# A binarised 3x3 convolution on 64x64 images: two output rows from four products, and the 3x3 sums of sizes on 64 partitions through memory

## What is computed

```python
def _L1_conv_ref(x, kernel, bias):             # x here is _gn(x): group norm
    xp = jnp.pad(x, ((0, 0), (1, 1), (1, 1), (0, 0)))
    bin_k = _sign_pm1(kernel)                  # 3 x 3 x 256 x 256, +1 or -1
    alpha = jnp.mean(jnp.abs(kernel), axis=(0, 1, 2))
    bin_x = _sign_pm1(xp)                      # v > 0 gives +1, else -1
    beta = jnp.mean(jnp.abs(xp), axis=3, keepdims=True)
    K = lax.reduce_window(beta, 0.0, lax.add, (1, 3, 3, 1), (1, 1, 1, 1), 'VALID') / 9
    conv = lax.conv_general_dilated(bin_x, bin_k, window_strides=(1, 1), padding='VALID', ...)
    return conv * (K * alpha) + bias
...
x = x + _L1_conv_ref(_gn(x), L1_conv_kernel, L1_conv_bias)
```

## Time and profile before

| | |
|---|---|
| median of 3 runs | 4247.38 us (4243.71 to 4248.18) |
| the profiled execution | 4246.04 us, span 4244.2 us |
| layer 1 in the span | first DMA issued at 3553.4 us, to the end |
| TensorE, VectorE, ScalarE, GpSimd busy, whole span | 3872.8, 3561.1, 2423.4, 569.8 us |

### The profile page before, as it was taken

The page is one execution under the profiler, slowest core; times in us unless marked ns, Lnnn a source line. Parts: engine busy times, 40 slices in busy tenths (PEclk is TensorE's granted clock), DMA queues, the critical chain, the costliest instruction groups (busy, mean ns, idle before and its releaser), DMA issues. The chain is left out here.

```text
span 4244.2 us, 94584 instructions
## 1 busy us (share of the span) xinstructions
PE 3872.8 (91%) x38382; PEld 2480.9 (58%) x38382; DVE 3561.1 (84%) x2896; ACT 2423.4 (57%) x5027; POOL 569.8 (13%) x480
## 2 busy tenths in 40 slices
PE   3899999999999999999999999999999985888988
PEld 1466666666666666666666666666666663333333
DVE  2799899989998899899989998999899993556554
ACT  4666666666666666666666666666666622333332
POOL 0011111111111111111111111111111110222222
PEclk9999999999999999999999999999999996999999
DMA  4454455445544554555445544554454433222321
GB/s 129 108 115 100 101 126 123 99 103 119 120 100 104 120 119 99 109 123 119 99 101 125 124 99 101 121 129 99 100 106 104 79 57 133 89 90 90 136 92 60
DMA packets 308092, 453.20 MB, mean 107 GB/s; under 512 B 33456, under 2 KB 239024, under 8 KB 301872
## 3 DMA queue, kind: packets, MB, share of 16 engines
q0 software_dynamic: 95168, 197.15, 25.9%
q1 hardware_dynamic: 212464, 249.71, 19.4%
HBM read 245.38 MB, written 67.11 MB: 74 GB/s over the span
## 5 line engine op out<-in xcount | busy, mean ns | idle before, releaser
L982 DVE TENSOR_TENSOR pv<-val,wsum 128x2048 f32<-128x2048 f32 x800 | 1810.3, 2283 | 11.1 <-PE ps_add L791 11.0
L791 PEld LDWEIGHTS ps_add<-ident,pv 128*128 128x128 f32 x12800 | 1399.7, 142 | 325.7 <-issue 220.7
L791 PE MATMUL ps_add<-ident,pv 128*128 128x128 f32 x12800 | 1525.0, 275 | 39.5 <-DVE pv L982 31.0
L746 PE MATMUL ps_om<-xdw,omw 128*32 128x256 f32 x13824 | 884.4, 389 | 124.7 <-ACT hat L579 109.1
L746 PEld LDWEIGHTS ps_om<-xdw,omw 128*32 128x32 f32 x13824 | 395.0, 111 | 431.7 <-ACT hat L579 120.8
L470 POOL DMA_DIRECT2D wsum<-prod x192 | 226.0, 1255 | 2688.6 <-DVE wsum L935 2688.6
L577 ACT ACTIVATE hat<-ps_om,omb 128x256 f32<-128x256 f32 x576 | 275.4, 478 | 537.0 <-PE ps_om L746 537.0
L935 DVE TENSOR_TENSOR prod<-hat,mwy 128x1536 f32<-128x1536 f32 (+1 forms) x384 | 525.2, 1395 | 59.0 <-DMA wsum<-prod 42.5
L1530 PE MATMUL ps_c<-c_sgn,c_ksgn 128*128 128x512 bf16 x2304 | 518.7, 384 | 2.5 <-DVE c_res L1647 2.5
L542 ACT ACTIVATE tri<-tri,gn_tri 96x512 f32<-96x512 f32 (+3 forms) x812 | 473.5, 647 | 6.0 <-DMA tri<-in_zeros_dram 0.5
L921 DVE TENSOR_TENSOR mwy<-hat,msk 128x768 f32<-128x768 f32 x288 | 274.1, 952 | 223.7 <-ACT hat L591 223.5
(11 more groups left out here) (102 smaller groups left out, 2791.2 us busy)
## 6 DMA issues: line engine op xcount, KB each, us to landing
wsum<-prod POOLq DMA_DIRECT2D x160, 768.0 KB, 6.9
tri<-in_x_dram SPq DMA_DIRECT2D x725, 128.0 KB, 2.9
win<-in_x_dram SPq DMA_DIRECT2D x144, 256.0 KB, 3.3
xres<-in_x_dram POOLq DMA_DIRECT2D x128, 256.0 KB, 9.0
x<-xres SPq DMA_DIRECT2D x128, 256.0 KB, 4.1
c_x<-x SPq DMA_DIRECT2D x8, 4096.0 KB, 13.0
out_dram<-c_x SPq DMA_DIRECT2D x32, 1024.0 KB, 4.0
acc<-in_x_dram POOLq DMA_DIRECT2D x14, 1024.0 KB, 5.6
```

The source lines that it names most:

```text
L746: mm = nc.tensor.matmul(ps_om[G * q:G * q + G, (par + i) % 2, 0:TOK], omw[:, h, comp, :], xdw[:, j % 2, h, q, :], start=h == 0, stop=h == ...
L791: mm = nc.tensor.matmul(ps_add[:, tb, c, :], pv[:, (j + uv) % PBUF, c, P * tb:P * tb + P], consts["ident"][:, :], start=uv == 0 and c % 4 ...
L982: nc.vector.tensor_tensor(pv[:, (j + uv) % PBUF, :, :].rearrange("p c (r w) -> p c r w", w=W), val[:, :, SR * j + u:SR * j + u + SR, v:v + ...
```

## The change

Only `layer1` changes. Three things go together.

**Products.** Two output rows are made of four products in place of six (for each column tap and input half). For a pair of output rows, the four input rows d0 to d3 give four planes: d0 - d2 and d1 - d3 (`over2`), d1 + d2 and d2 - d1 (`mid`, SUM and DIFF). They are made on VectorE in bf16 (`planes`), and weighed with four sets of weights `kw` that are made once. The products of `mid` are wanted in both rows with different signs: TensorE writes them to PSUM (`middle`, 12 matmuls), ScalarE copies them to `res`, one with its sign turned (`keep_middle`), TensorE then adds the outer products onto what stands in PSUM (`outside`, 12 matmuls), and VectorE adds `res` and PSUM (`combine`). The multiplication with `box` is a step of its own (`weigh`).

**Units.** A chunk is 16 rows (8 pairs, 1024 pixels); an image has 4 chunks and 8 units. `ps_p` has 3 slots of 2 banks, `res` 5 buffers. Loads, stores and signs go by chunk; `sgn` holds one image, and `planes` copies what the products read. All images are written out, with no loop.

**Sizes.** `mean_size` runs twice an image. It takes 8 products with 32 output channels each, four to different groups of 32 partitions of one bank, and adds the two halves itself (no `add_halves`). One partition of each group then holds 8 rows of the image's mean sizes. Four DMAs store them to a padded image in memory (`store_beta`), three DMAs load it back as 64 rows on 64 partitions, shifted by 0, 1 and 2 rows (`load_rows`), VectorE makes the sums in four steps of 66 or 64 elements (`box_sums`), a DMA stores the result, and another spreads it to 128 partitions (`spread_box`, 2 MB).

```diff
+    PAIRS = 8
+    CHUNKS = H // (2 * PAIRS)
+    CT = 2 * PAIRS * W
     UNITS = CHUNKS * CH
-    BANKS = 4
+    SLOTS, RES = 3, 5
...
+                def store_beta(n, half):
+                    sp.wait_ge(beta_out, 2 * n + half + 1)
+                    for i in range(BLOCKS):
+                        r0 = 1 + BW // W * (BLOCKS * half + i)
+                        sp.dma_start(beta_d[n % 2:n % 2 + 1, r0:r0 + BW // W, 1:1 + W],
+                                     beta[32 * i:32 * i + 1, half, :].rearrange("p (r w) -> p r w", w=W)).then_inc(beta_stored, 16)
+                def load_rows(n):
+                    sp.wait_ge(beta_stored, 16 * 2 * BLOCKS * (n + 1))
+                    for dr in range(3):
+                        sp.dma_start(rows[:, dr, :], beta_d[n % 2, dr:dr + H, :]).then_inc(rows_loaded, 16)
...
+                for n in range(NI):
+                    more = n + 1 < NI
+                    store_chunk(n, 0)
+                    if more:
+                        store_beta(n + 1, 0)
+                    refill(n, 0)
+                    if more:
+                        store_beta(n + 1, 1)
+                        load_rows(n + 1)
+                    store_chunk(n, 1)
+                    if more:
+                        store_box(n + 1)
+                    refill(n, 1)
+                    if more:
+                        spread_box(n + 1)
...
+                def keep_middle(i):
+                    act.wait_ge(mid_full, i + 1)
+                    if i >= RES:
+                        act.wait_ge(added, i - RES + 1)
...
+                    nc.scalar.activation(v[:, :, 0, :], total, ACT.Copy)
+                    nc.scalar.activation(v[:, :, 1, :], diff, ACT.Copy, scale=-1.0).then_inc(mid_kept, 1)
...
+                for i in range(UNITS * NI):
+                    n, u = i // UNITS, i % UNITS
+                    more = n + 1 < NI
+                    for w in weighed_at(i):
+                        affine(w)
+                    if more and u < 2:
+                        sizes(n + 1, u)
+                    if i + 1 < UNITS * NI:
+                        keep_middle(i + 1)
+                    if more and u in (2, 3):
+                        sizes(n + 1, u)
+                    if more and u in (2, 4):
+                        keep_beta(n + 1, u // 2 - 1)
...
+                def middle(i):
+                    n, u = i // UNITS, i % UNITS
+                    pe.wait_ge(v_made, 3 * (CHUNKS * n + u // CH + 1))
+                    if i >= SLOTS:
+                        pe.wait_ge(rows_done, i - SLOTS + 1)
+                    plane(n, u, DIFF, ps_p[:, i % SLOTS, 0, :], False)
+                    plane(n, u, SUM, ps_p[:, i % SLOTS, 1, :], False).then_inc(mid_full, 1)
+                def outside(i):
+                    n, u = i // UNITS, i % UNITS
+                    pe.wait_ge(mid_kept, i + 1)
+                    plane(n, u, FIRST, ps_p[:, i % SLOTS, 0, :], True)
+                    plane(n, u, LAST, ps_p[:, i % SLOTS, 1, :], True).then_inc(rows_full, 1)
...
+                for i in range(UNITS * NI):
+                    if i + 1 < UNITS * NI:
+                        middle(i + 1)
+                    outside(i)
+                    if i // UNITS + 1 < NI and i % UNITS in (2, 4):
+                        mean_size(i // UNITS + 1, i % UNITS // 2 - 1)
...
+                for n in range(NI):
                     for u in range(UNITS):
                         i = UNITS * n + u
+                        for w in weighed_at(i):
+                            weigh(w)
+                        if n == 0 and u == 2:
+                            box_sums(0)
+                        if u == 0:
+                            planes(n, CHUNKS - 1)
+                        elif n + 1 < NI:
+                            if u <= CHUNKS:
+                                signs(n + 1, u - 1)
+                            if u == 5:
+                                box_sums(n + 1)
+                            if u >= 5:
+                                planes(n + 1, u - 5)
+                        combine(i)
```

More of the change, by code:

```diff
@@ L1367, in layer1 @@
         xb = sb("c_x", [P, 2, CH, HW])
[L1368 to L1377, removed]
+        sgn = sb("c_sgn", [P, CH, PAD, PAD], BF16)
+        over2 = sb("c_over2", [P, CHUNKS, CH, 2 * PAIRS, PAD], BF16)
+        mid = sb("c_mid", [P, CHUNKS, 2, CH, PAIRS, PAD], BF16)
+        kw = sb("c_kw", [P, 4, CH, 3, C], BF16)
+        size = sb("c_size", [P, CH, HALF])
+        beta = sb("c_beta", [P, 2, BW])
+        rows = sb("c_rows", [H, 3, PAD])
+        down = sb("c_down", [H, PAD])
+        box_rows = sb("c_box_rows", [H, W])
+        box = sb("c_box", [P, 2, HW])
+        res = sb("c_res", [P, RES, CT])
         mean256 = sb("c_mean", [P, P])
@@ L1389, in layer1 @@
[L1389 to L1410, removed]
+        spare = xb[:, 1, :, :].rearrange("p h t -> p (h t)")
@@ L1499, in _ @@
+                affine(UNITS * NI - 1)
             @block.tensor
@@ new lines, in plane @@
+                def plane(n, u, which, at, more):
+                    t, oh = u // CH, u % CH
+                    for h in range(CH):
+                        for kx in range(3):
+                            if which in (SUM, DIFF):
+                                src = mid[:, t, which, h, :, kx:kx + W]
+                            else:
+                                r0 = 0 if which == FIRST else 1
+                                src = over2[:, t, h, r0:2 * PAIRS:2, kx:kx + W]
+                            first, last = h == 0 and kx == 0, h == CH - 1 and kx == 2
+                            mm = nc.tensor.matmul(at.rearrange("p (r w) -> p r w", w=W), kw[:, which, h, kx, P * oh:P * oh + P],
+                                                  src, start=first and not more, stop=last, skip_group_check=True)
+                    return mm
@@ new lines, in _ @@
+                pe.wait_ge(kern_step, KERN_STEPS)
+                middle(0)
+                pe.wait_ge(alpha_kept, 1)
+                for oh in range(CH):
+                    for i in range(2):
+                        mm = nc.tensor.matmul(ps_b[:, 0, oh:oh + 1], alpha[:, C * i + P * oh:C * i + P * oh + P],
+                                              mean256[:, 0:1], start=i == 0, stop=i == 1)
+                mm.then_inc(alpha_full, 1)
+                pe.wait_ge(scale_made, 1)
+                for half in range(2):
+                    mean_size(0, half)
```

388 lines of the change are left out of this document (199 added, 189 removed).

## The result

The changed kernel takes 4035.07 us (median of 4, 4028.21 to 4037.11) against 4246.31 for the one before: ratio 0.950, 95% interval 0.9484 to 0.9517, 211 us less. The prediction said 4042, 4000 to 4112. The profiled execution spans 4026.4 us and took 4028.21.

What follows compares the result with a forecast made beforehand. TensorE sets the second layer's pace: 3596.5 + 64 x 5.24 + 14 x 1.9, plus stops of 11.5 + 11.6 + 5 x 7.9, gives 4021; the end makes 4034, clock 6 and 1.8 around the span 4042 us, range 4000 to 4112.

Steps and rivals of the forecast that it cites:

- The choice between the two bounds: VectorE's `planes`: 4.6 us at float32 two-input pace or 2.4 at `c_ksgn`'s pace; the forecast took 2.4.
- a turn of 6.04 us: Port shared by VectorE and GpSimd, in units making planes: weigh 1.22 + planes 2.42 + GpSimd 2.4, against TensorE's 5.24.
- the one behind `sizes`: TensorE's 3.1 us wait in the unit where weigh, affine, both `sizes` and the copies follow each other.
- the one at unit 5: TensorE's 2.2 us wait for `combine`, queued on VectorE behind `box_sums`, which stands 7.2 us for the memory trips.
- the one in unit 6: TensorE's 1.0 us wait in unit 6, from the port turn.
- the two of 0.8: TensorE's 0.8 us waits: for `keep_middle` in the previous image's last unit with planes, and in unit 1 behind GpSimd.
- the clock's 6 us: TensorE's lower clock after gaps of 3 us, one an image: half of 1.7 us may come back, +6 in all.
- Slower planes: Rival: `planes` on VectorE at one element a cycle, port turn 8.3 us, image about 66 us, total 4135; chance 0.08.
- Slow memory trips: Rival: each small DMA lands in 4 us rather than 2, adding 4 us an image, total 4070; chance 0.10.
- No lock: Rival: the lock between VectorE and GpSimd costs nothing, as GpSimd falls between the steps; total 4014; chance 0.05.
- No overlap of the array's quarters: Rival: `mean_size` products on TensorE's array quarters don't overlap, about 10 us an image, total 4115; chance 0.02.
- A low clock throughout: Rival: TensorE stays at 1.2 GHz, a matmul 0.436 us, an image 87.5, the whole 4300; chance 0.02.

Runs made afterwards that it cites:

- run 1: Changed kernel with the 3x3 sums (`box_sums`) at unit 6 of VectorE's program, not unit 5: 4008.69 us, ratio 0.9447.
- run 2: Changed kernel with ScalarE's copies (`keep_middle`) ahead of the two `sizes` steps in units 0 and 1, not behind them: 4015.32 us, ratio 0.9459.
- run 7: Changed kernel with GpSimd adding only 64 of a unit's 1024 elements, the rest of the residual left out: 4004.89 us, ratio 0.9431.
- run 9: Changed kernel with each chunk's planes made once more in row order, into a spare place nobody reads: 4139.95 us, ratio 0.9757.
- run 4: Changed kernel with the middle products made twice, so 36 matmuls a unit as before the change: 4148.08 us, ratio 0.9776.
- run 5: Changed kernel without sizes and their sums for images 1 to 7, all weighed with the first image's sums: 3958.02 us, ratio 0.9324.
- run 6: Kernel before the change without sizes and their sums for images 1 to 7, using the first image's sums: 4116.16 us, ratio 0.9687.

## Why the prediction was right

The mechanism came out: TensorE still sets the pace, its products cost what was said, and an image loses the rest in the stops that were named, for the reasons that were named. That the total lies within 7 us is in part luck, since the start and the images were wrong in opposite directions.

**TensorE's terms.** The forecast had 24 matmuls a unit at 0.218 us. A piece of 12 stands at 2.78 to 2.85 us with its drain, and the next starts 2.62 after it; 48 in a row take 10.69. `mean_size` was two calls of 1.9 us and is 1.85 and 1.90 in the chain. Right.

**VectorE's terms.** `combine` was 1.22 (1.216 measured), `weigh` alone 1.22 (1.22 to 1.23). The planes were 0.62 + 0.62 + 1.18 = 2.42; from the first one's start to the start of `combine` behind them are 2.40 (3762.19 to 3764.59). The choice between the two bounds, by bytes read per ns, came out. The Trainium skill's page "VectorE: DVE Perf Modes" (The perf-mode tier table) has this rate, and the trace now shows it: 2112 elements in 1.25 us.

**The port.** Forecast was a turn of 6.04 us, with `weigh` stretched and `combine` not. Measured is 5.71. From the last plane's end to the addition's end are 2.21 us and not its 2.36, from there to `weigh`'s end 1.08 and not 1.22, and the next plane starts 0.08 before that end: each step saves some 0.1 us by following another. The mechanism was right and the term 0.3 us too large.

**An image.** Forecast was 53.6 us; by the starts of `mean_size` in the chain, 3676.28 and 3940.89, five images are 264.6 us, 52.9 each. Of the stops in the list, the one behind `sizes` was 3.1 and is 2.50, the one at unit 5 was 2.2 and is 1.65 to 1.77, the one in unit 6 was 1.0 and is 0.64, and the two of 0.8 are 0.24 each, or one of them none. That is 5.0 to 5.4 read off. But idle time is counted from the drain's end, so a stop costs 0.23 more than it reads (2.85 against 2.62), and the stops come to some 6.0 to 6.5 where 7.9 was said. The port's shorter turn is one cause. It is not the cause at unit 5, where VectorE stands for `c_rows`: there the mean sizes land in 1.7 us and not 2.0, and it stands 6.8 to 6.9 where 7.2 was said. Runs 1, 2 and 7 show that the sums, the copies and the port each count.

**The first image.** The forecast gave the first two images losses of 11.5 and 11.6 us. Measured, nearly all of it falls on one: from the first `mean_size` for the second image (3611.7) to the first for the third (3676.3) are 64.6 us, some 19 above its own work, and the next period has the 52.4 of the others. Half of it is the stop of 9.4 us that is shown with the profile, and the lower clock behind it about 4; run 1, in which that stop is 4.1 us, has 58.1. The forecast gave the memory trips 7.2 us in every image and did not see that in the first one they stand in the queue behind a store and a load that waits for it. The two together lose some 26 us, of which about 4 are the clock's, where 23 was said without the clock.

**The start was too small.** From the layer's first DMA to the stream of units were 43.1 us in the forecast (3596.5 - 3553.4) and are 47.2 measured (3595.2 - 3548.0). The weights landed in 10.45 (11 said), and the steps on VectorE took 9.8 (10.0). What was missed is TensorE's low clock, where the sum used full speed:

```profile
3573.72 5.28 PE L1614 MATMUL ps_p<-c_mid,c_kw 128*128 128x512 bf16 x12 [6.90 <-DVE c_over L1688]
...
3583.01 3.38 PE L1599 MATMUL ps_b<-c_size,c_mean 128*32 128x512 f32 x16 [1.29 <-ACT c_size L1528]
```

The granted clock from 3540 to 3595 is 0.59. The rows take 5.28 us in place of 2.6 and 3.38 in place of 1.9, and the second `mean_size` 3.64: 6 us more, of which the other terms, too large together, took back 2. In the earlier trace rows the same effect stood in plain sight, and the sum priced it only for the images.

**The clock in the images.** The forecast allowed 6 us, by the earlier trace rows, whose stop it read as some 4 us (3.07 in the row) and whose low clock as about 2 us long; the 1.7 us lost are right, but they need a longer low clock than 2 us (the granted clock is 0.50 from 3885 to 3888 there). About 6 us in all came out, but not for the reason given, which is luck: they were to be spread over all images. Measured, about 4 us come in the first image, behind its stop of 9.4 us (5.01, 4.06 and 3.27 us for pieces of 2.8). Of the five images after it, three last 52.4 to 52.5 us and two 53.6: in those two the stop of 2.5 us is followed by 12 matmuls in 4.25 and 4.47 us. That is 1.1 us twice.

**The sum.** Forecast for layer 1 with the clock's 6 us: 486.6; measured 478.4. It was too large in the units by 13.5 (430.5 against 417.0, from 3595.2 to the last matmul's end at 4012.2), too small at the start by 4.1 and by 1 at the end. Of the 13.5, 2.6 are a slip: the first middle products stand in the start's sum and again among the 64 units. Most of the rest are the stops. The median lies 7 us below the forecast, as what is left of errors of opposite sign.

**The rivals.** Slower planes: not so (run 9 has about the price). Slow memory trips: not as a rule, for the small DMAs landed in 2.0 us; but the reason given for this rival, one queue with 1 MB transfers, is seen in the first image, where VectorE stands 11.0 us in place of 6.9. No lock: false, and its price, 28 us, was measured as 30 in run 7, of which some 2 are the last addition's own. No overlap of the array's quarters: false, a call takes 1.9 us and not 9.9. A low clock throughout: false, it is 0.97 to 1.00 from 3703 to 3969. What the forecast did not say is how the 211 us divide; runs 4 to 6 do.

## What to carry to other kernels

When a change cuts the work of the engine that sets the pace, walk the other engines' in-order programs through one whole period with rows' durations: the two waits that were found that way on paper (copies queued behind independent work, and sums queued ahead of independent work) were worth 43 us, and moving two steps undid them. Walk the first period by itself: here it held the longest stop, 9.4 us against 2.5 in the later ones. An engine's idle share does not say how much more work it can take: 10 us an image on VectorE, idle for 14, cost 13. A DMA that is issued later in an in-order queue delays all that stands behind it, and a large one slows its followers; count them too.

## What the runs showed of the hardware

A two-input bf16 step on VectorE with neighbouring elements a row (132 bytes) apart takes 4.7 ns an element, against 0.59 with elements side by side (1.25 us for 2112); I had expected 1.1. Why it is so much, no run here tells.

Between GpSimd's addition and VectorE's steps with two inputs in SBUF the exclusion works both ways and by whole instructions: an addition of 2.36 us reads 3.27 when a plane is under way, and a `weigh` of 1.22 reads 2.13 during an addition. `combine`, with one input in PSUM, is not touched: its 64 rows in the changed kernel lie between 1.206 and 1.223 us.
